# Other orders in the routing, the expert network and the end of a convolution, attention and mixture-of-experts kernel

## What is computed

```
t = _to_tokens(x)                            # 2 x 1024 tokens of 128 channels
t = t + _L1_attn_ref(_ln_t(t), ...)
t = t + _L1_ffn_ref(_ln_t(t), ...)

def _L1_ffn_ref(x, Wr, br, W1, b1, W2, b2, gamma, beta):
    logits = jnp.mean(x, axis=1) @ Wr + br          # one row of 8 experts for each image
    routing_weights = softmax(logits)
    expected_loads = routing_weights.sum(axis=0) * (N / B)
    scale = jnp.where(expected_loads > capacity, capacity / expected_loads, 1.0)
    routing_weights = softmax(routing_weights * scale)
    top_w, top_i = jax.lax.top_k(rw_tok, 2); top_w = softmax(top_w)
    h = gelu(x @ W1[e] + b1[e]); y = h @ W2[e] + b2[e]
    out = sum over the two experts of top_w * y
    return layer_norm(out + x, gamma, beta)
```

## Time and profile before

| | |
|---|---|
| median of 3 runs | 413.36 us |
| the profiled execution | 413.38 us, of which the span from the first to the last instruction is 411.6 us |
| PE (TensorE) busy | 394.4 us, 96% |
| DVE (VectorE) | 311.7 us, 76% |
| ACT (ScalarE) | 296.7 us, 72% |
| POOL (GpSimd) | 96.5 us, 23% |
| mean granted TensorE clock | 0.998 of full speed |
| normalisation 1 of image 1 to the top-2 indices | about 355 to 370.5 us |
| expert network | about 371.5 to 399.4 us |
| last normalisation and output | about 399.4 to 411.6 us |

### The profile page before, as it was taken

How to read it: one execution, slowest core, us unless ns; L and a number is a source line. 1 busy time by engine, 2 the same in 40 slices (tenths; PEclk the granted TensorE clock), 3 DMA queues, 4 the chain that set the end, 5 groups by cost and what they waited for, 6 DMA issues and landing times.

```text
span 411.6 us, 5629 instructions
## 1 busy us (share of the span) xinstructions
PE 394.4 (96%) x1906; PEld 302.4 (73%) x1906; DVE 311.7 (76%) x701; ACT 296.7 (72%) x577; POOL 96.5 (23%) x94
## 2 busy tenths in 40 slices
PE   8899899999999999999999899999999999997995
PEld 3579795578777888888886688888888766645772
DVE  2798936668888988988899788898899265557745
ACT  1566664558788998999888899899898301457980
POOL 7300013111221520220220242662420000124015
PEclk9999999999999999999999999999999999999999
DMA  7990000000000000000000190000000000000002
GB/s 275 383 304 1 2 2 0 2 1 0 2 1 2 1 0 2 1 0 2 0 0 2 37 375 2 0 0 2 1 2 0 0 2 0 2 0 1 1 2 102
DMA packets 5262, 15.51 MB, mean 38 GB/s; under 512 B 690, under 2 KB 1906, under 8 KB 4978
## 3 DMA queue, kind: packets, MB, share of 16 engines
q1 hardware_dynamic: 4802, 14.19, 9.5%
q10 hardware_dynamic: 432, 0.97, 0.6%
HBM read 14.08 MB, written 1.08 MB: 37 GB/s over the span
## 4 chain that ended last, share of the span: by engine, by line
PE 81%; DVE 8%; ACT 8%; issue 3%; POOLq 0%; POOL 0%; ACTq 0%; DVEq 0%
PE ps L1061 12%; PE ps L1063 12%; PE ps L1062 12%; PE ps L1045 11%; PE ps L1153 7%; PE ps L810 4%; DVE nmax_all L1504 3%; PE ps L990 2%; PE ps L940 2%; PE ps L997 2%; PE ps L910 2%; PE ps L981 2%; PE ps L961 1%; ACT exps L691 1%; ACT qT_hi L681 1%
## 5 line engine op out<-in xcount | busy, mean ns | idle before, releaser
L1504 DVE TENSOR_REDUCE nmax_all<-ps 128x1 f32<-128x1024 f32 x128 | 156.7, 1224 | 8.2 <-PE ps L1063 6.6
L691 ACT ACTIVATE exps<-ps,nmax_all 128x1024 bf16<-128x1024 f32 x128 | 143.4, 1133 | 17.9 <-DVE diag_all L1509 17.3
L1061 PE MATMUL ps<-qT_hi,kT_hi 128*128 128x512 f32 x256 | 104.7, 409 | 2.8 <-ACT exps L691 1.3
L1063 PE MATMUL ps<-qT_hi,kT_lo 128*128 128x512 f32 x256 | 99.8, 390 | 0.0
L1062 PE MATMUL ps<-qT_lo,kT_hi 128*128 128x512 f32 x256 | 99.7, 390 | 0.0
L475 POOL TENSOR_TENSOR qT_lo<-xq,qT_hi 128x1024 fp32r<-128x1024 f32 x16 | 38.3, 2395 | 168.7 <-ACT xq L681 168.7
L1061 PEld LDWEIGHTS ps<-qT_hi,kT_hi 128*128 128x128 f32 x256 | 48.0, 188 | 16.5 <-ACT exps L691 2.9
L1045 PE MATMUL ps<-xn,wqkv 128*128 128x342 f32 (+3 forms) x256 | 58.2, 379 | 0.1
L1062 PEld LDWEIGHTS ps<-qT_lo,kT_hi 128*128 128x128 f32 x256 | 48.1, 188 | 10.9 <-issue 0.2
L1063 PEld LDWEIGHTS ps<-qT_hi,kT_lo 128*128 128x128 f32 x256 | 48.1, 188 | 10.3
L1045 PEld LDWEIGHTS ps<-xn,wqkv 128*128 128x128 f32 x256 | 42.6, 189 | 11.7 <-issue 0.9
(11 more groups left out here) (214 smaller groups left out, 552.1 us busy)
## 6 DMA issues: line engine op xcount, KB each, us to landing
xs_first<-a_store SPq DMA_DIRECT2D x4, 512.0 KB, 5.3
xs_second<-a_store SPq DMA_DIRECT2D x4, 512.0 KB, 8.4
wqkv<-laid_qkv_weights SPq DMA_DIRECT2D x1, 1536.0 KB, 6.2
wvT<-laid_qkv_weights_T SPq DMA_DIRECT2D x1, 1536.0 KB, 9.5
xq<-laid_x_queries SPq DMA_DIRECT2D x2, 512.0 KB, 6.3
xk<-laid_x_keys SPq DMA_DIRECT2D x2, 512.0 KB, 7.7
x<-in_x SPq DMA_DIRECT2D x1, 1024.0 KB, 12.4
w<-in_L_ffn_W SPq DMA_DIRECT2D x1, 1024.0 KB
```

The lines of the kernel that those rows point to most:

```text
L691: a.activation(exps[:, n % 2, :], slot(job_slot(("score", u, n))), ACT.Exp, bias=nmax_all[:, col:col + 1], accum_out=sum_all[:, col:col + ...
L1061: mm(tgt, keys_hi, qT_hi[:, u % 2, at], start=True, stop=False)
L1063: last = mm(tgt, keys_lo, qT_hi[:, u % 2, at], start=False, stop=True)
L1504: v.tensor_reduce(nmax_all[:, col:col + 1], slot(place), AX_X, ALU.max, negate=True)\
```

## The change

- Expert network: `second_layer` is called for each expert, and VectorE runs hidden_remainder(0) inside that of image 0's second expert, behind its b1 copy and ahead of its w2. b1 has a semaphore of its own (`b1_ready`). `hidden(0)` on TensorE issues its four matmuls on `w1_hi` before it waits for `w1_lo`. GpSimd waits for `y_ps` to reach 1 (outputs(0) done) before it makes w1 of image 1.
- Image 1's second normalisation: VectorE centres chunks 2 and 3 ahead of normalise(1, 1); chunks 2 and 3 have a root and a reciprocal each; several `keep_warm` are gone, shorter or moved; on ScalarE chunk_mean(3) goes ahead of round_tokens(2).
- Routing: the logit biases come ahead of the logits; pairs of small multiplications become one with a broadcast operand, and the capacity scale has one instruction less.
- End: diagonal 2 and the last addition of chunk 2 go from GpSimd to VectorE; residual(3) goes ahead of reciprocals(2, 0); three fillers ahead of the spreads are gone.

```diff
-        LN_PARTS = [((0, 1), (2, 3)), ((0, 1), (2, 3)), ((0, 1), (2,), (3,))]
+        LN_PARTS = [((0, 1), (2, 3)), ((0, 1), (2,), (3,)), ((0, 1), (2,), (3,))]
@@ gpsimd
             for b in range(2):
+                if b:
+                    pool.wait_ge(y_ps, 1)
                 for k in range(TOPK):
...
-            for c in range(3):
-                pool.wait_ge(LN[2]["rstd"], 1 if c < 2 else 2)
+            for c in range(2):
+                pool.wait_ge(LN[2]["rstd"], 1)
...
-            for c in range(3):
+            for c in range(2):
                 pool.wait_ge(LN[2]["out"], c + 1)
@@ scalar
             square(1, 3)
             round_tokens(1)
             root(1, 1, 0)
+            root(1, 2, 6)
             load_table(ACT.Exp)
             add_beta(1)
             chunk_mean(2)
+            chunk_mean(3)
             round_tokens(2)
-            chunk_mean(3)
             round_tokens(3)
...
-                act.wait_ge(w2_ready, 4 * (b * TOPK + k) + 1)
+                act.wait_ge(b1_ready, b * TOPK + k + 1)
@@ tensor
             spread(1, 1, 7)
-            keep_warm(2, 4)
             pe.wait_ge(t1_ready, 6)
             channel_means(1, 2, t1, "mean", 4)
             channel_means(1, 3, t1, "mean", 5)
-            keep_warm(2, 5)
+            keep_warm(2, 3)
             variances(1, 1, 0, 2)
-            variances(1, 1, 0, 3)
+            variances(1, 2, 6, 3)
...
-            keep_warm(2, 3)
             pe.wait_ge(ffn_in, 64)
+            logit_biases(0)
             logits(0)
             logits(1)
-            logit_biases(0)
+            keep_warm(7, 2)
             pe.wait_ge(LN[1]["diagonal"], 3)
             spread(1, 2, 1)
             pe.wait_ge(LN[1]["diagonal"], 4)
             spread(1, 3, 3)
-            keep_warm(0, 6)
+            keep_warm(0, 3)
+            logit_biases(1)
             logits(2)
-            logits(3)
-            logit_biases(1).then_inc(lg_ps, 1)
+            logits(3).then_inc(lg_ps, 1)
...
-                pe.wait_ge(w1_ready, 2 * (b * TOPK + k) + 2)
+                pe.wait_ge(w1_ready, 2 * (b * TOPK + k) + (2 if n else 1))
...
-                    mm(tgt, w1_lo[:, b, k, of], xn_hi[:, at], start=False, stop=True).then_inc(h_ps, 1)
+                    if n:
+                        mm(tgt, w1_lo[:, b, k, of], xn_hi[:, at], start=False, stop=True).then_inc(h_ps, 1)
+                if n == 0:
+                    pe.wait_ge(w1_ready, 2)
+                    for f in range(FC):
+                        mm(bank(f), w1_lo[:, b, k, f * P:(f + 1) * P], xn_hi[:, at], start=False, stop=True)\
+                            .then_inc(h_ps, 1)
...
             variances(2, 2, 0, 3)
-            keep_warm(3, 3)
-            for c in range(3):
+            for c in range(2):
                 pe.wait_ge(LN[2]["diagonal"], c + 1)
                 spread(2, c, 1 + c)
-            pe.wait_ge(last_diagonal, 1)
-            spread(2, 3, 4)
+            for c in (2, 3):
+                pe.wait_ge(last_diagonal, c - 1)
+                spread(2, c, 1 + c)
@@ vector
             normalise(1, 0, 6, xn, mb[:, 0:1])
-            normalise(1, 1, 7, xn, mb[:, 1:2])
             dve.wait_ge(t1_ready, 6)
             centre(1, 2, t1, 4)
             centre(1, 3, t1, 5)
+            normalise(1, 1, 7, xn, mb[:, 1:2])
 
             reciprocals(1, 1)
             lay_diagonal(1, 2, LN[1]["diagonal"])
+            reciprocals(1, 2)
             lay_diagonal(1, 3, LN[1]["diagonal"])
...
-                for b in range(2):
-                    v.tensor_scalar(rt[:, out_at, b, :], rt[:, e_at, b, :], rs_[:, col + 1, b:b + 1], None,
-                                    ALU.mult).then_inc(dve_step, 1)
-                count[0] += 2
-                dve.wait_ge(dve_step, count[0])
+                step(v.tensor_tensor(rt[:, out_at, :, :], rt[:, e_at, :, :],
+                                     rs_[:, col + 1, :].rearrange("p (b o) -> p b o", o=1).broadcast_to([P, 2, E]),
+                                     ALU.mult))
...
-            step(v.tensor_scalar(rt[:, 4, 1, :], rt[:, 4, 0, :], float(N // 2), None, ALU.mult))
-            step(v.reciprocal(rt[:, 4, 0, :], rt[:, 4, 1, :]))
-            step(v.tensor_scalar(rt[:, 4, 1, :], rt[:, 4, 0, :], CAPACITY, 1.0, ALU.mult, ALU.min))
+            step(v.reciprocal(rt[:, 4, 1, :], rt[:, 4, 0, :]))
+            step(v.tensor_scalar(rt[:, 4, 0, :], rt[:, 4, 1, :], CAPACITY / float(N // 2), 1.0, ALU.mult, ALU.min))
...
-            second_layer(0)
+            second_layer(0, 0)
...
-            hidden_remainder(0)
+            second_layer(0, 1, 0)
+            second_bias(0)
             hidden_remainder(1)
-            second_layer(1)
-            for c in range(4):
-                if c < 3:
-                    hidden_remainder(2 * c + 2)
-                else:
-                    reciprocals(2, 0)
+            second_layer(1, 0)
+            second_layer(1, 1)
+            second_bias(1)
+            for c in range(3):
+                hidden_remainder(2 * c + 2)
                 residual(c)
-                if c < 3:
-                    hidden_remainder(2 * c + 3)
+                hidden_remainder(2 * c + 3)
+            residual(3)
+            reciprocals(2, 0)
             reciprocals(2, 1)
+            lay_diagonal(2, 2, last_diagonal)
             reciprocals(2, 2)
             lay_diagonal(2, 3, last_diagonal)
...
-            dve.wait_ge(LN[2]["out"], 4)
-            at = slice(3 * 512, 4 * 512)
-            v.tensor_tensor(conv_o[:, at], centred[:, at], x1[:, at], ALU.add).then_inc(out_ready[3], 1)
+            for c in (2, 3):
+                dve.wait_ge(LN[2]["out"], c + 1)
+                at = slice(c * 512, (c + 1) * 512)
+                v.tensor_tensor(conv_o[:, at], centred[:, at], x1[:, at], ALU.add).then_inc(out_ready[c], 1)
```

More of the change, by code:

```diff
@@ L285, in build @@
         mb_ready, lg_ps, r_in, r_exp = (sem(n) for n in ("mb_ready", "logits_ps", "r_in", "r_exp"))
-        idx_ready, w1_ready, w2_ready = sem("idx_ready"), sem("w1_ready"), sem("w2_ready")
+        idx_ready, b1_ready, w1_ready, w2_ready = (sem(n) for n in ("idx_ready", "b1_ready", "w1_ready", "w2_ready"))
         h_ps, h_full, h_sb, h_lo, y_ps = (sem(n) for n in ("h_ps", "h_full", "h_sb", "h_lo", "y_ps"))
@@ L1195, in logits @@
                 pe.wait_ge(mb_ready, c + 1)
-                mm(bank(2, b * E, (b + 1) * E), mbb[:, c, :], wr[:, :], start=c % 2 == 0, stop=False)
+                return mm(bank(2, b * E, (b + 1) * E), mbb[:, c, :], wr[:, :], start=False, stop=c % 2 == 1,
+                          skip_group_check=True)
             def logit_biases(b):
-                return mm(bank(2, b * E, (b + 1) * E), ones[0:1, :], br[:, :], start=False, stop=True)
-            keep_warm(2, 3)
+                mm(bank(2, b * E, (b + 1) * E), ones[0:1, :], br[:, :], start=True, stop=False, skip_group_check=True)
             pe.wait_ge(ffn_in, 64)
+            logit_biases(0)
             logits(0)
             logits(1)
-            logit_biases(0)
+            keep_warm(7, 2)
             pe.wait_ge(LN[1]["diagonal"], 3)
@@ L1239, in outputs @@
                 c = n // 2
-                pe.wait_ge(w2_ready, 4 * (b * TOPK + k) + 4)
+                pe.wait_ge(w2_ready, 3 * (b * TOPK + k) + 3)
                 if k == 0 and c >= 2:
@@ L1636, in _ @@
             step(v.tensor_tensor(rt[:, 4, 0, :], rt[:, 3, 0, :], rt[:, 3, 1, :], ALU.add))
-            step(v.tensor_scalar(rt[:, 4, 1, :], rt[:, 4, 0, :], float(N // 2), None, ALU.mult))
-            step(v.reciprocal(rt[:, 4, 0, :], rt[:, 4, 1, :]))
-            step(v.tensor_scalar(rt[:, 4, 1, :], rt[:, 4, 0, :], CAPACITY, 1.0, ALU.mult, ALU.min))
-            for b in range(2):
-                v.tensor_tensor(rt[:, 5, b, :], rt[:, 3, b, :], rt[:, 4, 1, :], ALU.mult).then_inc(dve_step, 1)
-            count[0] += 2
-            dve.wait_ge(dve_step, count[0])
+            step(v.reciprocal(rt[:, 4, 1, :], rt[:, 4, 0, :]))
+            step(v.tensor_scalar(rt[:, 4, 0, :], rt[:, 4, 1, :], CAPACITY / float(N // 2), 1.0, ALU.mult, ALU.min))
+            step(v.tensor_tensor(rt[:, 5, :, :], rt[:, 3, :, :],
+                                 rt[:, 4, 0:1, :].broadcast_to([P, 2, E]), ALU.mult))
             softmax_input(rt[:, 5, :, :], 3)
@@ L1659, in _, with second_layer @@
             dve.wait_ge(t1_beta, 2)
-            def second_layer(b):
-                for k in range(TOPK):
-                    n = b * TOPK + k
-                    e = dve.value_load(top_i[0:1, b, k:k + 1], min_val=0, max_val=E - 1)
-                    v.tensor_copy(b1s[:, b, k, :], b1_all[:, bass.ds(e, 1), :].rearrange("p o f -> p (o f)"))\
-                        .then_inc(w2_ready, 1)
-                    chosen = w2[:, bass.ds(e, 1), :, :].rearrange("p o f c -> p (o f c)")
-                    hi_, lo_ = (t_[:, b, k, :, :].rearrange("p f c -> p (f c)") for t_ in (w2_hi, w2_lo))
```

(24 more changed lines are left out.)

## The result

The changed kernel takes **416.17 us** (median of 7, 415.91 to 418.23) beside 413.03 for the kernel before (median of 7): a ratio of 1.0066, 95% interval 1.0041 to 1.009. That is slower, by 0.4 to 0.9%, and above my range of 412.1 to 415.3.

A forecast was written before the change was run, and what follows sets the result against it. Bound after 350 us by a serial VectorE and ScalarE chain up to the top-2 indices, then TensorE in the network, then spreads and a late VectorE addition. 1.35 + 0.10 + 0.25 - 0.95 = +0.75 us gave 414.1 us, range 412.1 to 415.3.

The forecast's parts named there:

- rival 3: Image 1's normalisation: fewer fillers leave TensorE idle 2.4 us, its clock falls, costing 3 us: 417 us; chance 0.04.
- Part 1: Image 1's second normalisation: later square and a diagonal held by GpSimd cost +1.35 us, between 0.6 and 1.5.
- part 2: Routing: fewer tiny instructions save 0.80 us, but an addition held by GpSimd takes it back; +0.10 us.
- The tiny addition: Routing: VectorE's small addition with two SBUF inputs is held 1.15 us, until GpSimd's remainders end.
- Rival 1: VectorE and GpSimd don't hold each other up in normalisation, routing, network and end: 411.7 us; chance 0.13.
- Part 3: Expert network: outputs(0) starts earlier, but VectorE's weights beside GpSimd's copies delay hidden_remainder(2); +0.25 us.
- Rival 2: Expert network: GpSimd's copies slow VectorE's image 1 weights by up to 1.6 us; 415.1 us; chance 0.17.
- Part 4: End: earlier residual(3), fewer fillers and work moved to VectorE save time; -0.95 us, between -0.7 and -1.15.

The follow-up runs named there:

- a2: The changed kernel with 12 fillers instead of 3 behind the channel means of chunks 2 and 3; 413.97 us, ratio 1.0009 to the kernel before.
- a4: The changed kernel with image 1's second normalisation (centring order, parts, fillers, ScalarE order) put back as before; 412.4 us, ratio 0.9959 to the kernel before.
- b2: The kernel before with only the change's routing edits; 412.52 us, ratio 0.9986 to the kernel before.
- b1: The kernel before with only the change's edits of the end; 412.54 us, ratio 0.9984 to the kernel before.

## Why the prediction was wrong

**The step that failed is rival 3, the clock, which the sum put at nothing.** I named it and its place, TensorE idle for 2.4 us in the normalisation with the fillers gone (measured 2.21), and its price of 3 us (measured 1.70 or 3.0 to 3.2). I gave it a chance of 0.04 and left it out of the range, because no row of before between 350 and 400 us showed a fall. But in before no idle time of TensorE is longer than 1.46 us there, nor longer than 1.52 anywhere: the rows could not speak on 2.4. The absence of a fall was no evidence against it, only the absence of a test. With its price the sum is 0.75 and 1.7 to 3.2, so 415.8 to 417.3, and 416.17 is in it. That it fits so well is partly luck: the other terms come to +0.14 in a2 (1.44 - 1.30), 0.6 less than my 0.75. The rule that I cited from the Trainium skill (TensorE: Matmul & The Clock Gate, Part 1), that idleness brings the clock to half, was borne out: 0.50 at 366 to 368 us, behind the 2.21 us, though the fall came only when TensorE was at work again.

**Part 1 without the clock and part 2: right.** Counted on before's clock (2.98 us of early shift taken off), the square of chunk 2 was at 359.34 where I had 359.5, and the root at 361.16 where I had 361.3. Diagonal 2 ended 0.55 us behind GpSimd's instruction, forecast 0.53. The tiny addition took 1.13 us where I had put its hold at 1.15. In a2, at the full clock, the first exponential comes 1.29 us later than in before, counted from the reciprocal (forecast for part 1: 1.35), and from there to the end of the indices it takes 0.15 more (forecast for part 2: 0.10); together +1.44, forecast +1.45. That agrees with the section "Who interferes with whom" of the Trainium skill (SBUF, State Buffer), now also for eight elements. Rival 1, independent engines, is refuted by the same rows.

What causes the sum divides otherwise than its place: part 1's order costs 2.02 (a2 less a4), and the routing alone gains 0.59. I had given the held addition to part 2, but it is part 1 that puts GpSimd's remainders onto it, since b2 shows the routing alone without it.

**Part 3: sign wrong, small.** Forecast +0.25, measured -0.14 (segment 2's -1.30 less the end's -1.16). The mis-sized step is GpSimd's company on the weights: on before's clock, counted from the end of the indices, image 1's weights started where I had them (379.32, forecast 379.35), but hidden_remainder(2) at 382.32 instead of 382.8. Image 1's pair of weights took 385.44 to 388.41, 2.97 us, near the 2.77 that it takes alone and far from the 4.40 of image 0's pair. Rival 2 had the right place and a wrong price: GpSimd's copies fell on these weights, as the rows at 384.69 and 385.44 show, and cost 0.2 us instead of up to 1.6. TensorE was idle ahead of outputs(2), 1.12 us, but it had been 1.46 in front of outputs(0) before.

**Part 4: mechanism right, size a little off.** Forecast -0.95 with bounds at -0.7 and -1.15, measured -1.16 in b1. In after the last residual starts at 405.38; without the 2.98 of early shift and the 3.0 that parts 1 to 3 and the clock added (3.14 - 0.14) that is 399.4, forecast 399.45. The first spread starts 2.41 us behind it, 3.00 in the earlier trace rows, and the last addition ends at 413.73, by the same reckoning 407.75, a little ahead of my 407.9 to 408.2.

## What to carry to other kernels

Fillers that look superfluous may be what holds TensorE's clock through a wait, and a profile in which the clock never fell says nothing of an idle time longer than any in it: price such a fall where the change makes a new, longer wait, and give it a chance that fits. Where a step is moved ahead on one engine, look at what stands ahead of its consumer on the next: here one mean in ScalarE's queue turned an earlier centring into a later square, and moving it was worth more than the fillers. And an instruction taken off GpSimd's collision with VectorE has to be followed to where it lands.
